# Text layers: scores in row groups of 64, gelu of two groups every second step, second norm one step later, variances on POOL

## The chip, the cores and the metric

The kernel runs on one core of a Trainium2 chip. The time is the device time of one execution in microseconds (us). A core has five engines that run side by side, each through its own list of instructions in order: PE (TensorE, matmuls; its weight loads are shown apart as PEld), DVE (VectorE), ACT (ScalarE), POOL (GpSimd) and SP (SyncE, here only transfers). They wait for each other by semaphores.

## What is computed

A block with four parts: an image branch (convolutions), a text branch of four transformer layers, then an attention over both and a layer of experts. The change touches only the text branch. Cut to that:

```python
L, H, D, F, V, S = (4, 8, 64, 256, 100, 512)
DH = D // H                       # 8
x = emb[tokens] + positional_encoding(Sq, D)[None]     # tokens (64, 77)
for i in range(L):
    q = (x @ Wq[i] + bq[i]).reshape(B, Sq, H, DH).transpose(0, 2, 1, 3)
    k = (x @ Wv[i] + bv[i]).reshape(B, Sq, H, DH).transpose(0, 2, 1, 3)
    v = (x @ Wv[i] + bv[i]).reshape(B, Sq, H, DH).transpose(0, 2, 1, 3)
    attn = jax.nn.softmax(jnp.einsum('bhqd,bhkd->bhqk', q, k) * scale, axis=-1)
    o = jnp.einsum('bhqk,bhkd->bhqd', attn, v).transpose(0, 2, 1, 3).reshape(B, Sq, D)
    x = x + layer_norm(o @ Wo[i] + bo[i], ln1_g[i], ln1_b[i])
    h = jax.nn.gelu(x @ W1[i] + b1[i], approximate=False)
    x = x + layer_norm(h @ W2[i] + b2[i], ln2_g[i], ln2_b[i])
return layer_norm(x, fin_g, fin_b)
```

## The kernel before

The function `text_branch` holds all of it. The 64 samples of 77 tokens are worked on in groups of four (`QUAD`), so 16 groups (`U`) and 4 layers make N = 64 pieces of work, numbered q. All of a group's activations stay in the core's memory.

**Heads.** The eight heads of 8 channels stand in two tensors (`t`), four heads in each; a head has 32 of the 128 rows (`GROUP` = 32, `HPT` = 4). In its 32 rows lie the channels in three parts (high and low parts of a split into two precisions) and a row for the maximum. To multiply one head alone with 128 rows, K is written four times by POOL (`split_k`, L1055) into `KB`, each copy with all rows but one head's set to zero (`head_rows` is the mask): 4 x 312 columns for each tensor.

**One sample's attention** is a chain over the engines: `score` (PE, L1318: two matmuls of 128 rows with 312 columns, four heads side by side) - `find_max` (DVE, L916, reads the scores from PSUM) - `turn_max` (PE, L1328, two transposes) - `join_max` (DVE, L926, puts the maximum into the rows of Q: `QP`) - `score_t` (PE, L1340: eight matmuls, one a head, 78 columns each) - `exp` (ACT, L1186) - `weigh` (PE, L1354: eight products with weights of 9 columns, placed in four column groups of the array; sixteen instructions in the profile) - `copy_outs` (ACT, L1192) - `turn_outs` (PE, L1362) - `normalise_o` (DVE, L936 and L938). `score` of the next sample waits for `find_max` of this one (one buffer), `weigh` of the next for `normalise_o` (one bank), `score_t` of the next for `exp`.

**Around it**, once a group: `hi_x`, `cut_x`, `turn_x` (L1261), `set_xT`, `project_k` (L1285), `project_q` (L1294), `project_v` (L1304), with `lo_k`, `lo_q` (ACT, L1170, L1177) and `cut_k`, `cut_q` (DVE, L886, L895) that split the results; `turn_o` (L1269), `project_o` (L1370, L1374), then the first norm: `square_a` (ACT), `var_a` (DVE: the sum L952 and the variance L956), `power_a` (POOL, L1079), `scale_a` (L947), `shift_a`, `sum_a` (L965). Then the feed-forward part: `hi_f`, `cut_f`, `turn_f` (PE, L1277), `set_fT`, `up` in two halves (PE, L1383), `gelu` in two halves (ACT, L1213), `down` (PE, L1393 and L1397), and the second norm in the same manner with `_y` (L980, L984, L1086, L975, L993).

**Order.** Each engine has a function `step(n)` in which the order is written out by hand; step n works on group n, n-1, ... n-5 at different points of the pipeline. There is no loop on the chip, all N + 5 steps are written out. ACT has to load a table before gelu and again before the next exp: two table loads in each step. PE's six projections share two PSUM banks:

```python
WORK = dict(x=1, k0=0, k1=1, q0=0, q1=1, v=1, o=0, a=0, f=1, up0=0, up1=1, y=0)
```

`take(use, read, q)` waits until the bank's last content was read: project_v and up of half 1 use bank 1, project_q of tensor 0 (read by `cut_q` on DVE) and up of half 0 use bank 0.

## Time and profile before

| | us |
|---|---|
| median of 3 runs | 2328.38 (2327.67 to 2330.51) |
| the profiled execution | 2329.04 |
| its span, first to last instruction | 2327.2 |

Busy over the whole span: PE 2091.1 (90%), DVE 1735.5 (75%), ACT 1419.1 (61%), POOL 1144.9 (49%). The text layers take the stretch from about 560 to 1445 us. "Idle before" in brackets is time in which the engine had nothing to run, and behind the arrow stands what ended it. Matmuls overlap, and their ends are modelled: the distance between the ends (start plus duration) of two neighbouring groups is the time that the later group takes up.

### The profile page before, as it was taken

The numbers are of one execution on the slowest core, as the hardware profiler recorded it, in microseconds if no ns is written. First come the engines' busy times: TensorE is split into PE (matmuls) and PEld (weight loads), VectorE is DVE, ScalarE is ACT, GpSimd is POOL, SyncE is SP. The second block draws the span as 40 slices with busy tenths as digits, with TensorE's granted clock in tenths as the row PEclk, the third lists the DMA queues.
The fourth block names the chain that finished last, engine by engine and source line by source line (L and its number), as shares of the span: only waits on it lengthen the run. The fifth ranks groups of instructions, "written<-read, shape, count | busy, mean of one in ns | idle before, by whom it ended". The sixth has DMA issues, their size and how long they took to land. (4 is left out here: it accounts for less than half of the span.)

```text
span 2327.2 us, 59267 instructions
## 1 busy us (share of the span) xinstructions
PE 2091.1 (90%) x20401; PEld 1720.2 (74%) x20401; DVE 1735.5 (75%) x5336; ACT 1419.1 (61%) x3034; POOL 1144.9 (49%) x1520
## 2 busy tenths in 40 slices
PE   5999999965999999999999997099999996999998
PEld 5999999954888888888888886066666664666665
DVE  4655555426788888888888885668888775888888
ACT  2222222211788888888888885466666665666663
POOL 4333333312577777777777774633333324343442
PEclk8999999975999999999999998589999996999999
DMA  2000003000000000000000000000000000000000
GB/s 91 16 15 14 14 14 81 13 1 0 2 3 2 3 2 3 2 3 2 3 2 3 2 3 1 0 1 2 2 2 2 2 1 3 10 9 9 9 9 11
DMA packets 38895, 21.14 MB, mean 9 GB/s; under 512 B 28696, under 2 KB 38040, under 8 KB 38554
## 3 DMA queue, kind: packets, MB, share of 16 engines
q1 hardware_dynamic: 38654, 17.97, 3.1%
q8 instruction: 146, 2.39, 0.4%
q14 instruction: 95, 0.78, 0.1%
HBM read 14.60 MB, written 3.36 MB: 8 GB/s over the span
## 5 line engine op out<-in xcount | busy, mean ns | idle before, releaser
L452 PE MATMUL im_c<-im_a_hi,im_w 128*128 128x256 f32 (+2 forms) x1920 | 427.0, 317 | 15.3 <-POOL im_a_lo L362 15.3
L452 PEld LDWEIGHTS im_c<-im_a_hi,im_w 128*128 128x128 f32 x1920 | 320.5, 190 | 32.4 <-POOL im_a_lo L362 15.5
L452 PE MATMUL im_c<-im_a_lo,im_w 128*128 128x256 f32 (+2 forms) x960 | 302.8, 315 | 0.0
L1055 POOL TENSOR_TENSOR tx_KB<-tx_KF,tx_head_rows 128x1248 fp32r<-128x1248 f32 x128 | 290.0, 2265 | 23.2 <-PE tx_scores_t L1340 15.2
L356 POOL TENSOR_TENSOR im_rstd<-im_var_eps,im_power 128x4 f32<-128x4 f32 x64 | 68.7, 1073 | 282.9 <-DVE im_var_eps L291 282.9
L916 DVE TENSOR_REDUCE tx_mpad<-tx_scores 77x8 fp32r<-77x616 f32 x256 | 202.1, 789 | 2.8 <-PE tx_maxT L1328 1.9
L285 DVE BATCH_NORM_STATS2 im_stats<-im_h 128x6 f32<-128x128 f32 (+1 forms) x192 | 47.6, 303 | 189.8 <-ACT im_h L397 110.7
L452 PEld LDWEIGHTS im_c<-im_a_lo,im_w 128*128 128x128 f32 x960 | 182.2, 190 | 8.3
L1186 ACT ACTIVATE tx_PT<-tx_scores_t 77x624 f32<-77x624 f32 x256 | 176.1, 688 | 16.8 <-PE tx_scores_t L1340 4.6
L1340 PE MATMUL tx_scores_t<-tx_QP,tx_KB 128*77 128x78 f32 x2048 | 183.9, 240 | 0.0
L1340 PEld LDWEIGHTS tx_scores_t<-tx_QP,tx_KB 128*77 128x77 f32 x2048 | 172.4, 150 | 9.1 <-issue 0.3
L2379 PE MATMUL ex_y<-ex_wd,ex_H_hi 128*128 128x512 f32 (+1 forms) x512 | 171.7, 416 | 0.0
L1768 DVE TENSOR_REDUCE at_mpad<-at_scores 128x4 fp32r<-128x820 f32 (+1 forms) x128 | 129.5, 1012 | 43.3 <-PE at_scores L1988 43.2
L1854 POOL TENSOR_TENSOR at_xs<-at_z,at_xs 128x128 fp32r<-128x128 f32 x64 | 29.4, 460 | 245.4 <-ACT at_xs L1871 245.4
L391 ACT ACTIVATE im_a_hi<-im_normed 128x192 fp32r<-128x192 f32 (+1 forms) x192 | 63.1, 349 | 139.3 <-DVE im_normed L309 137.0
L1047 POOL TENSOR_TENSOR tx_xs_f<-h,tx_xs_f 77x256 fp32r<-77x256 f32 x64 | 46.7, 730 | 199.9 <-ACT tx_xs_f L1136 199.9
L2268 DVE TENSOR_REDUCE ex_summed<-ex_weighted 128x64 f32<-128x512 f32 (+1 forms) x128 | 135.5, 1059 | 4.4
L1578 POOL TENSOR_TENSOR ex_rstd<-ex_var_eps,ex_power 128x2 f32<-128x2 f32 x64 | 44.6, 697 | 181.2 <-DVE ex_var_eps L1543 181.2
L1903 ACT ACTIVATE at_PT<-at_scores_t 128x824 f32<-128x824 f32 (+1 forms) x128 | 109.7, 857 | 30.7 <-PE at_scores_t L2011 26.9
L1318 PE MATMUL tx_scores<-tx_KB,tx_QF 128*77 128x312 f32 x512 | 126.0, 327 | 1.3 <-DVE tx_mpad L916 1.2
L1354 PE MATMUL tx_out_bank<-tx_PT,tx_V 128*9 128x78 f32 x4096 | 118.0, 233 | 9.2 <-DVE tx_o_rows L938 2.3
L362 POOL TENSOR_TENSOR im_a_lo<-im_normed,im_a_hi 128x192 fp32r<-128x192 f32 (+1 forms) x192 | 93.7, 518 | 52.4 <-ACT im_a_hi L391 52.4
(321 smaller groups left out, 6062.3 us busy)
## 6 DMA issues: line engine op xcount, KB each, us to landing
im_x<-x SPq DMA_DIRECT2D x16, 384.0 KB, 3.3
out<-h SPq DMA_DIRECT2D x32, 64.0 KB
tx_toks<-x_txt SPq DMA_DIRECT2D x1, 1925.0 KB
im_raw<-L_tok_conv_w SPq DMA_DIRECT2D x1, 1280.0 KB, 8.5
out<-h SPq DMA_DIRECT2D x32, 38.5 KB
im_raw<-L_tok_conv_w SPq DMA_DIRECT2D x1, 960.0 KB, 4.6
im_raw<-L_tok_conv_w SPq DMA_DIRECT2D x1, 640.0 KB, 5.8
tx_raw_W<-L_txt_W SPq DMA_DIRECT2D x2, 256.0 KB, 6.7
```

What stands on the lines that cost most here:

```text
L362: last = pool.tensor_tensor(a_lo[c][:, par, b, :, 2:2 + J], normed[:, b, 0:cols * J].rearrange("p (d j) -> p d j", d=cols), a_hi[c][:, par ...
L452: last = pe.matmul(acc[:, :, d0:d1], w[c][:, slot, part], img[:, b0_:b1_, d0 + shift:d1 + shift, kj:kj + J], start=opens, stop=closes)
L916: dve.tensor_reduce(mpad[0:R].rearrange("p t (j r) -> p t j r", r=GROUP)[:, :, :, 3 * DH], scores[0:R, :, 0:HPT * SP_TXT].rearrange("p t ( ...
L1055: pool.tensor_tensor(KB[:, q % 2, t], KF[:, t].bitcast(F32).unsqueeze(1).broadcast_to([P, HPT, QW]), head_rows[:].unsqueeze(2).broadcast_t ...
L1186: act.activation(PT[0:R, b % 2], scores_t[0:R, :, 0:HPT * SP_TXT], ACT.Exp, scale=SCALE)\
L1318: last = pe.matmul(scores[0:R, t, 0:HPT * SP_TXT], QF[:, q % 2, t, b, 0:R], k, start=True, stop=True)
L1340: last = pe.matmul(scores_t[0:R, t, j * SP_TXT:(j + 1) * SP_TXT], k, QP[:, b % 2, t], start=True, stop=True)
L1354: last = pe.matmul(outT[32 * j:32 * j + DH + 1, t], V[:, q % 2, b, t * HPT + j], PT[:, b % 2, t, j * SP_TXT:(j + 1) * SP_TXT], start=True, ...
L1768: dve.tensor_reduce(mpad[0:n, tile].rearrange("p t (j r) -> p j t r", r=A_GROUP)[:, :, :, 3 * A_DH], scores[0:n, :, 0:WIDE].rearrange("p j ...
L1903: act.activation(PT[0:n, tile], scores_t[0:n, :, 0:WIDE], ACT.Exp, scale=SCALE).then_inc(exped, 1)
L2268: dve.tensor_reduce(summed[0:n, tile], weighted[0:n, tile].rearrange("p e d -> p d e"), AX.X, ALU.add)\
L2379: last = pe.matmul(acc, h[:, slot, half, at:at + n], wd[:, part, half, 0:WIDE], start=False, stop=half == HALVES - 1 and h is H_lo)
```

## The change

1. `score` and `score_t` work with 64 of the 128 rows at a time (`ROWS` = 2 halves of `PAIR` = 2 heads). K is written twice instead of four times (`KB`, 2 x 312 columns). `score` is four matmuls of 64 rows with 156 columns, `score_t` eight of 64 rows with 78; halves `a` alternate and go to different banks. The layout of `scores`, `scores_t` and `PT` follows.
2. `up` and `gelu` are run for two groups (n-6 and n-5) in each even step and not at all in odd ones. `down` and the second norm move from n-5 to n-6; the pipeline has N + 6 steps.
3. The variances (`tensor_scalar` on 77x4) move from DVE to POOL (`var_eps_a`, `var_eps_y`), and two waits at the end of POOL's step go.

```diff
-        KB = sb("KB", [P, 2, TENSORS, HPT, QW], F32R)
-        PT = sb("PT", [P, 2, TENSORS, HPT * SP_TXT])
+        KB = sb("KB", [P, 2, TENSORS, PAIR, QW], F32R)
+        PT = sb("PT", [P, 2, ROWS, HPT * SP_TXT])
...
                         dve.wait_ge(a_squared, q + 1)
+                        if q >= 2:
+                            dve.wait_ge(a_var, q - 1)
                         dve.tensor_reduce(a_sums[:, q % 2], a_square[:, q % 2], AX.X, ALU.add).then_inc(a_summed, 1)
-                        dve.wait_ge(a_summed, q + 1)
-                        if q >= 2:
-                            dve.wait_ge(a_power, q - 1)
-                        dve.tensor_scalar(a_var_eps[:, q % 2], a_sums[:, q % 2], 1.0 / D, EPS, ALU.mult, ALU.add)\
-                            .then_inc(a_var, 1)
...
-                        pool.tensor_tensor(KB[:, q % 2, t], KF[:, t].bitcast(F32).unsqueeze(1).broadcast_to([P, HPT, QW]),
-                                           head_rows[:].unsqueeze(2).broadcast_to([P, HPT, QW]), ALU.mult)\
+                        pool.tensor_tensor(KB[:, q % 2, t], KF[:, t].bitcast(F32).unsqueeze(1).broadcast_to([P, PAIR, QW]),
+                                           head_rows[:].unsqueeze(2).broadcast_to([P, PAIR, QW]), ALU.mult)\
...
+                def var_eps_a(q):
+                    if live(q):
+                        pool.wait_ge(a_summed, q + 1)
+                        pool.tensor_scalar(a_var_eps[:, q % 2], a_sums[:, q % 2], 1.0 / D, EPS, ALU.mult, ALU.add)\
+                            .then_inc(a_var, 1)
...
-                    shift_y(n - 5)
+                    shift_y(n - 6)
                     cut_x(n)
                     split_k(n - 1, 0)
+                    var_eps_a(n - 4)
                     power_a(n - 4)
                     cut_o(n - 3)
-                    power_y(n - 5)
-                    let_sum_y(n - 5)
-                    let_sum_a(n - 4)
+                    var_eps_y(n - 6)
+                    power_y(n - 6)
...
                     lo_q(n - 1, 0)
-                    gelu(n - 5, 1)
-                    gelu(n - 5, 0)
+                    if n % 2 == 0:
+                        gelu(n - 6, 1)
+                        gelu(n - 6, 0)
+                        gelu(n - 5, 1)
+                        gelu(n - 5, 0)
...
                         for t in range(TENSORS):
-                            k = KB[:, q % 2, t].rearrange("p j (b s) -> p j b s", b=QUAD)[:, :, b]
-                            last = pe.matmul(scores[0:R, t, 0:HPT * SP_TXT], QF[:, q % 2, t, b, 0:R], k, start=True, stop=True)
+                            for a in range(ROWS):
+                                rows, wide = slice(a * P // ROWS, (a + 1) * P // ROWS), PAIR * SP_TXT
+                                k = KB[rows, q % 2, t].rearrange("p j (b s) -> p j b s", b=QUAD)[:, :, b]
+                                last = pe.matmul(scores[0:R, a, t * wide:(t + 1) * wide], QF[rows, q % 2, t, b, 0:R], k,
+                                                 start=True, stop=True)
...
                         for t in range(TENSORS):
-                            for j in range(HPT):
-                                k = KB[:, q % 2, t, j].rearrange("p (b s) -> p b s", b=QUAD)[:, b, 0:R]
-                                last = pe.matmul(scores_t[0:R, t, j * SP_TXT:(j + 1) * SP_TXT], k, QP[:, b % 2, t],
-                                                 start=True, stop=True)
+                            for j in range(PAIR):
+                                for a in range(ROWS):
+                                    rows, at = slice(a * P // ROWS, (a + 1) * P // ROWS), (t * PAIR + j) * SP_TXT
+                                    k = KB[rows, q % 2, t, j].rearrange("p (b s) -> p b s", b=QUAD)[:, b, 0:R]
+                                    last = pe.matmul(scores_t[0:R, a, at:at + SP_TXT], k, QP[rows, b % 2, t],
+                                                     start=True, stop=True)
```

PE's order, from project_q of tensor 0 (L1294, after the change L1296) to project_v (L1304, after it L1306). Before, in every step:

```order
L1294 MATMUL tx_work<-tx_xT,tx_w_all 128x312 x2
L1362 MATMUL tx_out_bank<-ident,tx_oU 77x128 x2
L1383 MATMUL tx_work<-tx_xTf,tx_w_all 128x312 x2
L1340 MATMUL tx_scores_t<-tx_QP,tx_KB 77x78 x8
L1318 MATMUL tx_scores<-tx_KB,tx_QF 77x312 x2
L1328 MATMUL tx_maxT<-ident,tx_mpad 128x77 x2
L1383 MATMUL tx_work<-tx_xTf,tx_w_all 128x312 x2
L1354 MATMUL tx_out_bank<-tx_PT,tx_V 9x78 x8
L1304 MATMUL tx_work<-tx_w_all,tx_xT 77x64 x8
```

PE's order in the same place after the change, in an even step (in an odd one the four rows of L1391, `up`, are not there):

```order
L1296 MATMUL tx_work<-tx_xT,tx_w_all 128x312 x2
L1370 MATMUL tx_out_bank<-ident,tx_oU 77x128 x2
L1391 MATMUL tx_work<-tx_xTf,tx_w_all 128x312 x2
L1347 MATMUL tx_scores_t<-tx_QP,tx_KB 77x78 x8
L1391 MATMUL tx_work<-tx_xTf,tx_w_all 128x312 x2
L1322 MATMUL tx_scores<-tx_KB,tx_QF 77x156 x4
L1333 MATMUL tx_maxT<-ident,tx_mpad 128x77 x2
L1391 MATMUL tx_work<-tx_xTf,tx_w_all 128x312 x2
L1362 MATMUL tx_out_bank<-tx_PT,tx_V 9x78 x8
L1391 MATMUL tx_work<-tx_xTf,tx_w_all 128x312 x2
L1306 MATMUL tx_work<-tx_w_all,tx_xT 77x64 x8
```

The second `up`, of half 0, has moved from behind `turn_max` to between `score_t` and `score`, and two more stand on either side of `weigh`.

POOL's order from the second `split_k` (L1055, after it L1052) to the end of the step, before (L1079 and L1086 are the powers, L1041 is `cut_o`):

```order
L1035 TENSOR_TENSOR tx_xs<-h,tx_xs 77x4x64
L1055 TENSOR_TENSOR tx_KB<-tx_KF,tx_head_rows 128x1248
L1079 TENSOR_TENSOR tx_a_rstd<-tx_a_var_eps,tx_power 77x4
L1041 TENSOR_TENSOR tx_os<-tx_o_rows,tx_os 77x4x64
L1086 TENSOR_TENSOR tx_y_rstd<-tx_y_var_eps,tx_power 77x4
```

After:

```order
L1032 TENSOR_TENSOR tx_xs<-h,tx_xs 77x4x64
L1052 TENSOR_TENSOR tx_KB<-tx_KF,tx_head_rows 128x624
L1074 TENSOR_SCALAR tx_a_var_eps<-tx_a_sums 77x4
L1082 TENSOR_TENSOR tx_a_rstd<-tx_a_var_eps,tx_power 77x4
L1038 TENSOR_TENSOR tx_os<-tx_o_rows,tx_os 77x4x64
L1087 TENSOR_SCALAR tx_y_var_eps<-tx_y_sums 77x4
L1095 TENSOR_TENSOR tx_y_rstd<-tx_y_var_eps,tx_power 77x4
```

Each power now has its variance right ahead of it on POOL, and the K product has half the columns.

## Rows read from the trace of the kernel before

**Rows 1.** Windows: from:to, length, busy PE PEld DVE ACT POOL, PEclk, DMA share, GB/s.
```profile
800.00:1000.00 200.00, 191.99 (x2670) 171.12 (x2670) 177.12 (x525) 177.56 (x361) 149.60 (x135) 1.00 0.01 2
...
800.94:814.28 13.34, 12.88 (x180) 11.48 (x178) 11.81 (x36) 11.85 (x25) 9.98 (x10) 1.00 0.01 4
```

**Rows 2.** Groups, 600 to 1380 us: count | busy us, mean ns | idle before.
```profile
L1055 POOL TENSOR_TENSOR tx_KB<-tx_KF,tx_head_rows 128x1248 fp32r<-128x1248 f32 x118 | 267.3, 2265 | 4.3 <-PE tx_scores_t L1340 4.3
...
L956 DVE TENSOR_SCALAR tx_a_var_eps<-tx_a_sums 77x4 f32<-77x4 f32 x58 | 54.7, 943 | 2.0
```

**Rows 3.** Time line of PE in one step (start us, duration us, group).
```profile
800.33 0.68 PE L1340 MATMUL tx_scores_t<-tx_QP,tx_KB 128*77 128x78 f32 x8
800.94 0.46 PE L1354 MATMUL tx_out_bank<-tx_PT,tx_V 128*9 128x78 f32 x16
801.33 0.49 PE L1277 MATMUL tx_work<-ident,tx_xs_f 77*128 77x77 f32 x4
801.62 0.50 PE L1318 MATMUL tx_scores<-tx_KB,tx_QF 128*77 128x312 f32 x2
801.95 0.30 PE L1328 MATMUL tx_maxT<-ident,tx_mpad 77*128 77x77 f32 x2
...
802.64 0.54 PE L1383 MATMUL tx_work<-tx_xTf,tx_w_all 128*128 128x312 f32 x2
803.01 0.68 PE L1340 MATMUL tx_scores_t<-tx_QP,tx_KB 128*77 128x78 f32 x8
803.57 0.52 PE L1318 MATMUL tx_scores<-tx_KB,tx_QF 128*77 128x312 f32 x2
803.93 0.30 PE L1328 MATMUL tx_maxT<-ident,tx_mpad 77*128 77x77 f32 x2
804.11 0.52 PE L1383 MATMUL tx_work<-tx_xTf,tx_w_all 128*128 128x312 f32 x2
...
805.29 0.71 PE L1304 MATMUL tx_work<-tx_w_all,tx_xT 128*77 128x64 f32 x8 [0.27 <-ACT tx_HT L1213]
...
806.64 1.26 PE L1397 MATMUL tx_work<-tx_w_all,tx_HT 128*77 128x64 f32 x16
807.74 0.44 PE L1261 MATMUL tx_work<-ident,tx_xs 77*128 77x77 f32 x4
808.28 0.46 PE L1354 MATMUL tx_out_bank<-tx_PT,tx_V 128*9 128x78 f32 x16
808.67 0.75 PE L1340 MATMUL tx_scores_t<-tx_QP,tx_KB 128*77 128x78 f32 x8
...
812.85 0.38 PE L1362 MATMUL tx_out_bank<-ident,tx_oU 128*77 128x128 f32 x2
813.31 0.53 PE L1285 MATMUL tx_work<-tx_xT,tx_w_all 128*128 128x312 f32 x2
```

**Rows 4.** Time line of DVE in the same step: join_max, find_max, cut_q.
```profile
802.29 0.32 DVE L926 TENSOR_TENSOR tx_QP<-tx_maxT,tx_QF 128x154 fp32r<-128x154 f32 x1 [0.30 <-PE tx_maxT L1328]
802.72 0.80 DVE L916 TENSOR_REDUCE tx_mpad<-tx_scores 77x8 fp32r<-77x616 f32 x1
803.44 0.53 DVE L895 SCALAR_TENSOR_TENSOR tx_QF<-tx_work,tx_cols_all,tx_qk_lo 128x312 fp32r<-128x312 f32 x1
```

**Rows 5.** Time line of ACT in the same step: table load and gelu.
```profile
803.33 1.28 ACT L1213 ACT_TABLE_LOAD   x1
804.63 0.93 ACT L1213 ACTIVATE tx_HT<-tx_work,tx_cols_all 128x312 f32<-128x312 f32 x2
```

**Rows 6.** Time line of PE in the attention stage: a 128-row group, then 64-row pairs.
```profile
1651.29 0.61 PE L72 MATMUL at_of_q<-warm_rows 128*128 128x512 bf16 x2
1651.83 0.42 PE L1988 MATMUL at_scores<-at_KF,at_QF 64*77 64x206 f32 x4
```

**Rows 7.** Groups of POOL: a variance of 128x2 elements in the attention stage.
```profile
L1837 POOL TENSOR_SCALAR at_var_eps<-at_mean_var 128x2 f32<-128x2 f32 x64 | 14.1, 220 | 5.0 <-DVE at_mean_var L1761 5.0
```

**Rows 8.** Time line of PE at the end of the text layers: the last down.
```profile
1439.54 2.26 PE L1397 MATMUL tx_work<-tx_w_all,tx_HT 128*77 128x64 f32 x16
```

60 lines of the change are left out of this document (33 added, 27 removed).

## The prediction

> **What bounds the kernel now.** I read the window table first. In the text layers, from about 600 to 1400 us, PE is busy for 96% of the time at a granted clock of 1.00, that is 2.4 GHz, and one step (one group of four samples in one layer) takes 13.34 us: PE 12.88, DVE 11.81, ACT 11.85, POOL 9.98 busy [rows 1]. There are 64 such steps. PE is the bound, but DVE and ACT have only some 1.5 us of air each, so PE's own time and its waits must both be followed. The change touches nothing outside this stage.
>
> Next, the time line of PE in one step [rows 3]. I take the distance between the ends of neighbouring groups (start plus duration). Call T0 the end of the last score_t of the step before, 801.01. Two things are to be seen. First, what the narrow matmuls of weigh (L1354, 128 x 9 weights, four side by side) cost when PE goes into and out of them. Four transposes after weigh end 0.42 after it (L1277), while four transposes after ordinary matmuls end 0.28 after them (L1261 after L1397): leaving the narrow form costs about 0.15 us. Second, few true waits: project_v (L1304) with 0.27 idle; weigh of sample 0 (L1354 at 808.28) ends 0.56 after the transposes, where 0.39 is normal, so 0.17 is a wait; project_k (L1285 at 813.31) ends 0.61 after its neighbour, where a pair of such matmuls behind transposes takes about 0.33 (0.30 to 0.40 for L1383), so 0.2 to 0.3 is a wait. With a tenth here and there I put PE's waits at 1.05 and its work at 12.29 us a step.
>
> **The change part by part: PE's work.** The form to be priced, two 64-row matmuls side by side, stands in the attention stage: after a 128-row group that ends at 1651.90, two pairs of 64 x 77 weights with 206 columns end at 1652.25, so 0.35 us including the way in [rows 6]. From it I work out, as estimates at 2.4 GHz: score (now two pairs of 156 columns instead of two matmuls of 312) 0.35 less twice 50 columns, 0.31, or 0.18 directly behind another 64-row group; score_t (now four pairs of 78 columns instead of eight matmuls) 0.35 plus two more weight loads of 0.07 (that is the spacing of the eight now: 0.51 for eight) less the shorter columns, 0.40. Today score_t ends 0.51 after an ordinary group and 0.68 after weigh (808.67), score 0.29 to 0.34 [rows 3]. So four score_t go from 2.24 to 1.62 (-0.62), and four score from 1.25 to 1.24, or 1.09 in a step where one follows score_t directly.
>
> Against that stand the ways out. Five groups in each step now follow a 64-row group and did not follow a change of form before (turn_max four times, turn_outs once); no row shows this way out, so I take the nearest, that out of weigh, 0.15; the one behind score_t saves 0.05 of it: +0.70. Its bounds are 0.08 and 0.2. Such a pair of prices (entry is in the 0.35 already) makes PE's work in an odd step 12.29 - 0.69 (no up) - 0.62 - 0.16 + 0.70, 11.52 us. In an even step there are four up instead of two: +0.76, of which 0.08 is because one stands between two 64-row groups; score and score_t -0.63; ways out +0.70; another 0.1 for the second group behind weigh: 13.22. The mean is 12.37, no less than the 12.29 of now. What the narrow rows save, the changes of form give back. The Trainium skill, page "TensorEngine Tiling (Array Packing)", section "Key Properties", says that a change of tiling mode (not just of tile) drains the TensorE; the trace agrees with the 0.15 us around weigh. The same page, section "Theoretical Speedup", has up to 2x for a contraction of 64 rows or less; taken alone it would take half of 3.49 us a step.
>
> **ACT, DVE, POOL.** The table loads (1.28 us each, two a step) are made every second step: ACT loses 1.28 us a step on average, but an even step has four gelu of 0.47 and both loads in one piece [rows 5]. POOL's KB product is half as long, 2.26 to about 1.2 us [rows 2], and that is worth nothing by itself: POOL is busy for only 9.98 of 13.34 us [rows 1]. The variance on DVE takes 0.94 us for 77x4 elements [rows 2], far over what such a thing needs, and it delays normalise_o and so weigh of sample 0: the 0.17 goes. On POOL it costs 0.22 [rows 7] twice; on y it stands ahead of power_y, for which sum_y waits: up to 0.2, in the even step.
>
> **The new waits, by a walk through a step.** In row order: turn_max of sample 0 ended at T0+1.24. After the change it ends at 1.45 (0.15 way out, 0.05 because DVE's find_max for sample 0 comes later: turn_outs before it ends 0.15 later and score_t 0.12 earlier). Then join_max starts 0.04 later, find_max of sample 1 starts 0.43 after that and takes 0.79, and PE may start score of sample 2 0.05 after its end [rows 4]: 1.49, 1.92, 2.71, 2.76. Today this is T0+2.56, exactly when PE starts it (803.57): there is no slack left on this chain now.
> In an odd step PE would be ready for score 2 at about 2.25, since there is no up and score_t is shorter. It waits 0.5. Behind find_max DVE has cut_q (0.45 to the next start) and normalise_o (0.44), so weigh of the last sample, which needs the output bank free, waits another 0.3. The wait at project_v goes, that at weigh 0 goes, that at project_k stays near 0.2. Waits 1.05, step 12.57.
> In an even step up of half 0 (bank 0, held until cut_q is done) stands ahead of score 2. cut_q ends at 2.64 + 0.53 = 3.17, up starts at 3.28, PE was ready at 2.75: 0.5 us. Then up of half 1 of the second group must wait for gelu of the first: lo_q, table load, gelu end at 4.35, up starts at 4.46, 0.2 late. weigh, up, project_v, down follow; exp of sample 0 comes behind four gelu, a copy and the second table load, at about 8.6, just when PE wants weigh 0 (8.66): nothing or 0.05. project_o 0.05, project_q 0.2 (sum_y behind power_y), project_k 0.2. Waits 1.29, step 14.51.
>
> **Sum.** Mean step (12.57 + 14.51) / 2 = 13.54 against 13.34: +0.20, times 64 is +13 us. The pipeline is one step longer: a further down at the low clock, 2.26 us [rows 8], and the variance on POOL, +2.5. Of the profiled execution (2329.04, span 2327.2) this makes 2344.5; against the median of 2328.38 it is **2344 us**, +0.7%. One wait misjudged by 0.15 us a step is 10 us, and the way out at 0.08 or 0.2 makes -22 or +16 us (5.5 of them a step), of which part goes into waits, since a later PE waits less: I halve it. Own range 2333 to 2363.
>
> **Rivals.**
> (1) Relief wins: faster, 0.27. In the walk the waits add up; if those behind the first one of a step lie under it (PE late at the first is no longer early at the next, since DVE and ACT have been given 1.1 and 1.28 us a step), then the even step keeps 0.5 us of waits and ends at 13.7, the odd one loses the wait at the last weigh and ends at 12.3: 13.0, -0.34 x 64 + 2.5, 2309. It decides once more than 0.24 us a step falls away of the 1.17 that I count. For it: the table loads and the 0.94 us variance are real, and ACT is 89% busy. Against: the chain turn_max, join_max, find_max has no slack now, and the change makes it longer.
> (2) They cancel: 13.30 a step, 2328, 0.13.
> (3) My forecast, slower by turning forms and the two new waits: 0.55.
> (4) The pairs don't run side by side in this stage, since score_t has weights of only 77 columns and 78 columns to move: score_t back at 0.51 plus the way in of 0.1, +0.8 a step, 2385: 0.04. Against it rows 6.
> (5) The matmuls of both kinds cost half and changes of form are hidden, as a mechanism of this kernel: 3.49 / 2 x 64, -112 us if nothing else waited, but the DVE chain would hold it: at best 12.3 a step (DVE 10.9 busy plus what it waits), 2265. 0.01. This is what the 2x of the Trainium skill, page "TensorEngine Tiling (Array Packing)", section "Theoretical Speedup", would make; no row of the trace shows it.
> A way out of the 64-row form of 0.05 us instead of 0.15 would bring the forecast down to no change.
>
> **Chances and range.** A measurement of this kernel tells about 0.2% (4.7 us) from no change. Slower 0.59 (3, 4), same 0.13, faster 0.28 (1, 5). The range, 2306 to 2368, takes in most of rival 1 and the bounds of the forecast.
>
> **What would show it.** PE's busy time near 96% with PE's groups turn_max behind score ending 0.28 to 0.30 after it instead of 0.13; score_t at 0.40 and four 64-row weight loads in pairs; odd and even steps of 12.6 and 14.5; idle time of PE ahead of score in odd steps put down to tx_mpad, and ahead of the first up of half 0 in even steps put down to tx_QF; no DVE variance, ACT busy near 80%. It is wrong if turn_max still ends 0.13 after score, or if the even step is under 13.8.

## The result, and the profile after

| | before | after |
|---|---|---|
| median, us | 2329.45 (2327.67 to 2333.0, 4 runs) | 2386.81 (2383.55 to 2391.64, 4 runs) |
| span of the profiled execution, us | 2327.2 | 2381.7 |

The ratio is 1.0246 (95% interval 1.0222 to 1.027): slower, by 57 us where the forecast had 16, and outside the range of 2306 to 2368. The ratios here and below compare fast runs with fast runs; one run of rows_pairs (2440.8 us) and one of rows_heat64_long (2365.8 us) were slow and are left out of theirs.

First the steady part: the window table of the changed kernel, with one odd and one even step on top, then three stretches that cover the start of the stage, then the first three steps one by one (columns as in [rows 1]):

```profile
831.11:843.74 12.63, 12.11 (x187) 9.71 (x183) 10.80 (x34) 8.44 (x21) 8.25 (x12) 1.00 0.01 2
843.74:858.45 14.71, 13.73 (x194) 10.87 (x190) 10.87 (x34) 12.56 (x27) 8.28 (x12) 1.00 0.01 2
...
561.00:591.00 30.00, 22.75 (x169) 17.05 (x169) 11.99 (x26) 12.41 (x24) 8.28 (x9) 0.50 0.00 1
591.00:620.00 29.00, 28.74 (x282) 23.28 (x281) 15.32 (x43) 13.27 (x28) 8.34 (x11) 0.50 0.00 1
620.00:673.00 53.00, 52.87 (x467) 42.81 (x467) 27.87 (x79) 28.23 (x57) 21.78 (x28) 0.50 0.01 2
...
624.00:641.61 17.61, 17.48 (x169) 13.95 (x165) 9.45 (x28) 8.81 (x20) 6.44 (x9) 0.50 0.01 3
641.61:664.00 22.39, 22.39 (x195) 18.33 (x191) 10.98 (x34) 13.95 (x27) 8.33 (x12) 0.50 0.01 1
664.00:679.60 15.60, 15.60 (x186) 12.89 (x182) 10.24 (x33) 8.27 (x21) 7.26 (x11) 0.70 0.01 2
```

An odd step takes 12.63 us and an even one 14.71 (14.72 in most), a mean of 13.675; the forecast had 12.57, 14.51 and 13.54. The two lower blocks are what the forecast did not speak of at all: TensorE's granted clock is 0.50 (1.2 GHz) from 561 to 673 us, while PE is busy for 28.74 of 29 and 52.87 of 53 us. The first two of these stretches in the kernel before:

```profile
561.00:591.00 30.00, 22.56 (x144) 19.24 (x148) 11.38 (x26) 11.53 (x23) 11.12 (x7) 0.50 0.00 1
591.00:620.00 29.00, 26.86 (x382) 23.55 (x375) 21.87 (x61) 20.32 (x44) 19.71 (x16) 1.00 0.01 2
```

There the clock goes to 1.00 (2.4 GHz) at 591.2, 82 us earlier. PE's time line at the end of this stage in the kernel before:

```profile
1447.03 0.77 PE L1277 MATMUL tx_work<-ident,tx_xs_f 77*128 77x77 f32 x4 [5.23 <-POOL tx_xs_f L1047]
...
1450.76 2.26 PE L1397 MATMUL tx_work<-tx_w_all,tx_HT 128*77 128x64 f32 x16
```

I mark a step by its first turn_f (four transposes of `tx_xs_f`); the first one of all starts at 614.7 before and at 624.0 after, and the last at 1447.03 and at 1496.31. The last sum_y (DVE adds the second norm of the last group) ends at 1456.1 and at 1510.9. So the 54.5 us between the two spans divide up like this:

| part of the text stage | us |
|---|---|
| up to the first turn_f, at half clock for longer | 9.3 |
| the first three steps, 17.61 + 22.39 + 15.60 against 3 x 13.33 | 15.6 |
| the other 60 steps: 56 at +0.34 (19), one of them with a short fall of the clock (1.6 more), and the last four, where the pipeline empties (4.1) | 24.4 |
| from the last turn_f to the last sum_y, 14.6 against 9.1 | 5.5 |
| the stages after | -0.3 |

The time line of PE in the changed kernel: pieces of the odd and of the even step, and the end of the stage (start, duration, group):

```profile
831.11 0.49 PE L1279 MATMUL tx_work<-ident,tx_xs_f 77*128 77x77 f32 x4
831.66 0.37 PE L1322 MATMUL tx_scores<-tx_KB,tx_QF 64*77 64x156 f32 x4
831.96 0.35 PE L1333 MATMUL tx_maxT<-ident,tx_mpad 77*128 77x77 f32 x2
832.20 0.52 PE L1296 MATMUL tx_work<-tx_xT,tx_w_all 128*128 128x312 f32 x2
832.56 0.38 PE L1370 MATMUL tx_out_bank<-ident,tx_oU 128*77 128x128 f32 x2
832.87 0.47 PE L1347 MATMUL tx_scores_t<-tx_QP,tx_KB 64*77 64x78 f32 x8
833.43 0.38 PE L1322 MATMUL tx_scores<-tx_KB,tx_QF 64*77 64x156 f32 x4
...
834.46 0.46 PE L1362 MATMUL tx_out_bank<-tx_PT,tx_V 128*9 128x78 f32 x16 [0.37 <-DVE tx_o_rows L941]
...
845.79 0.47 PE L1347 MATMUL tx_scores_t<-tx_QP,tx_KB 64*77 64x78 f32 x8
846.72 0.53 PE L1391 MATMUL tx_work<-tx_xTf,tx_w_all 128*128 128x312 f32 x2 [0.46 <-DVE tx_QF L897]
856.10 0.52 PE L1296 MATMUL tx_work<-tx_xT,tx_w_all 128*128 128x312 f32 x2 [0.31 <-DVE tx_KF L888]
...
1501.60 2.26 PE L1405 MATMUL tx_work<-tx_w_all,tx_HT 128*77 128x64 f32 x16
1505.20 0.47 PE L1401 MATMUL tx_work<-tx_w_all,tx_ones 128*77 128x256 f32 x1 [1.34 <-DVE tx_y_scaled L975]
1505.47 2.25 PE L1405 MATMUL tx_work<-tx_w_all,tx_HT 128*77 128x64 f32 x16
```

And DVE's find_max just ahead of the first of these scores:

```profile
830.82 0.79 DVE L918 TENSOR_REDUCE tx_mpad<-tx_scores 77x8 fp32r<-77x616 f32 x1
```

Read as ends of neighbouring groups: turn_max ends 0.28 behind score (832.03, 832.31), where it was 0.13 in [rows 3]; score_t ends 0.40 behind the transposes (832.94, 833.34). The score of sample 2 ends 0.47 behind score_t, where the prediction's estimate is 0.18 without a wait. So it waits 0.29, and the forecast had 0.5. Another 0.13 stands one score earlier: that of sample 1 ends 0.43 behind turn_f (831.60, 832.03) instead of 0.30, and starts 0.05 behind the end of find_max (831.61). weigh of the last sample (834.46) waits 0.37 for normalise_o, where the forecast had 0.3. In the even step the first up of half 0 (846.72) waits 0.46 for cut_q (forecast 0.5), and project_q (856.10) waits 0.31 for cut_k (forecast 0.2). ACT is busy for 21.0 of the 27.34 us of the two steps, 77%; the forecast had near 80.

### The profile page after: what moved, and what is told of

It reads as the page before. It is cut to its first block and busy times, and to the rows that moved or that the text cites. A ratio compares the mean times of both kernels' runs of the same rounds, so it can differ in the third digit from the quotient of the medians.

```text
span 2381.7 us, 60100 instructions
## 1 busy us (share of the span) xinstructions
PE 2130.4 (89%) x20849; PEld 1680.4 (71%) x20913; DVE 1676.5 (70%) x5208; ACT 1338.8 (56%) x2972; POOL 1034.6 (43%) x1648
## 5 line engine op out<-in xcount | busy, mean ns | idle before, releaser
L1052 POOL TENSOR_TENSOR tx_KB<-tx_KF,tx_head_rows 128x624 fp32r<-128x624 f32 x128 | 156.8, 1225 | 27.7 <-PE tx_scores_t L1347 17.9
L1362 PE MATMUL tx_out_bank<-tx_PT,tx_V 128*9 128x78 f32 x4096 | 123.0, 240 | 12.2 <-DVE tx_o_rows L941 10.9
L1347 PE MATMUL tx_scores_t<-tx_QP,tx_KB 64*77 64x78 f32 x2048 | 125.8, 250 | 0.3 <-DVE tx_QP L929 0.2
L1347 PEld LDWEIGHTS tx_scores_t<-tx_QP,tx_KB 64*77 64x77 f32 x2048 | 95.0, 151 | 40.0 <-issue 22.2
L1176 ACT ACTIVATE tx_qk_lo<-tx_work,tx_cols_all,tx_lo_rows 128x312 fp32r<-128x312 f32 x128 | 78.2, 611 | 67.9 <-PE tx_work L1296 64.0
```

Source lines behind the costliest of these rows:

```text
L1052: pool.tensor_tensor(KB[:, q % 2, t], KF[:, t].bitcast(F32).unsqueeze(1).broadcast_to([P, PAIR, QW]), head_rows[:].unsqueeze(2).broadcast_ ...
L1176: act.activation(qk_lo[:, t], bank(f"q{t}")[:, 0:QW], ACT.Identity, bias=col(q, 2 + t), scale=lo_rows[:, 0:1]).then_inc(q_lo_[t], 1)
L1347: last = pe.matmul(scores_t[0:R, a, at:at + SP_TXT], k, QP[rows, b % 2, t], start=True, stop=True)
L1362: last = pe.matmul(outT[32 * j:32 * j + DH + 1, t], V[:, q % 2, b, t * HPT + j], PT[:, b % 2, j // PAIR, at:at + SP_TXT], start=True, stop ...
```

## The experiments

The steady step, in us, is the distance between turn_f in the trace of each kernel; times are medians of all runs of a kernel. R is part 1 of the change (row groups of 64), P part 2 (two groups every second step, second norm six steps behind), V part 3 (variances on POOL). Ratios are to the kernel before, run beside each; its own median moved between the sets of runs, from 2328.7 to 2333.4 us, so compare ratios and not times.

| kernel | step odd / even | mean | time, us | ratio, 95% interval |
|---|---|---|---|---|
| before | 13.33 | 13.33 | 2329.45 | 1 |
| rows_only (R) | 13.10 | 13.10 | 2334.6 | 1.0012 (1.0 to 1.0024) |
| var_only (V) | 13.74 | 13.74 | 2352.48 | 1.0089 (1.007 to 1.0109) |
| pairs_only (P) | 13.27 / 14.43 | 13.85 | 2367.2 | 1.0146 (1.0127 to 1.0166) |
| rows_var (R, V) | 13.10 | 13.10 | 2328.54 | 1.0004 (0.9981 to 1.0027) |
| rows_pairs (R, P) | 12.63 / 14.56 | 13.60 | 2414.15 | 1.035 (1.0278 to 1.0422) |
| pairs_var (P, V) | 13.75 / 14.56 | 14.15 | 2391.85 | 1.0252 (1.0231 to 1.0272) |
| after (all) | 12.63 / 14.72 | 13.68 | 2386.81 | 1.0246 (1.0222 to 1.027) |
| rows_heat | 13.10 | 13.10 | 2330.04 | 1.0004 (0.9994 to 1.0014) |
| before_heat | 13.33 | 13.33 | 2326.16 | 0.9983 (0.9974 to 0.9993) |
| after_heat | 12.63 / 14.72 | 13.68 | 2403.18 | 1.0327 (1.0298 to 1.0355) |
| rows_heat64 | 13.10 | 13.10 | 2332.65 | 1.0015 (1.0006 to 1.0025) |
| rows_heat_long | 13.10 | 13.10 | 2329.18 | 0.9976 (0.995 to 1.0002) |
| after_up0 | 12.63 / 14.72 | 13.68 | 2386.22 | 1.0239 (1.0194 to 1.0283) |
| rows_heat_both | 13.10 | 13.10 | 2329.01 | 0.9981 (0.997 to 0.9993) |
| before_heat_both | 13.33 | 13.33 | 2348.61 | 1.0024 (0.9991 to 1.0056) |
| after_heat_long | 12.63 / 14.72 | 13.68 | 2376.77 | 1.0209 (1.0141 to 1.0277) |
| rows_heat64_long | 13.10 | 13.10 | 2318.21 | 0.9937 (0.9915 to 0.9959) |
| rows_heat64_long again | 13.10 | 13.10 | 2322.52 | 0.9938 (0.9915 to 0.9962) |
| after_short_gelu | 12.63 / 14.34 | 13.49 | 2391.75 | 1.024 (1.0206 to 1.0274) |

### The parts one by one

Part 1 alone. The edit is every line of the change on `KB`, `head_rows`, `PT`, score, score_t and find_max; the order of work is that of before.

```diff
-        KB = sb("KB", [P, 2, TENSORS, HPT, QW], F32R)
+        KB = sb("KB", [P, 2, TENSORS, PAIR, QW], F32R)
...
+                            for a in range(ROWS):
+                                rows, wide = slice(a * P // ROWS, (a + 1) * P // ROWS), PAIR * SP_TXT
```

> The kernel before with the first part of the change alone: 64-row groups in score and score_t, half the K product; orders, gelu and variances as before. Theory A: it is the 64-row matmuls that keep TensorE at its 1.2 GHz level longer at the start of the text layers (after the change it rose at 673 us, before at 591). Then the clock rises late here too, between 650 and 690 us, which costs 20 to 30 us, and the steady step is 13.3 to 13.6 us: 2350 to 2375 us. Theory B: the late clock comes from the uneven steps (up and gelu every second step). Then it rises near 591 us here and the time is 2328 to 2345.

Windows of this kernel, one steady step, then the start of the stage:

```profile
810.57:823.66 13.09, 12.83 (x187) 10.25 (x187) 11.11 (x36) 11.86 (x25) 7.91 (x10) 1.00 0.02 4
...
591.00:620.00 29.00, 28.75 (x283) 23.21 (x282) 14.83 (x44) 13.41 (x29) 7.06 (x8) 0.50 0.00 1
620.00:673.00 53.00, 51.96 (x669) 41.73 (x669) 39.86 (x124) 44.13 (x86) 29.47 (x34) 0.86 0.01 2
```

Two of its groups from 640 to 1380 us (count | busy us, mean ns | idle before):

```profile
L1058 POOL TENSOR_TENSOR tx_KB<-tx_KF,tx_head_rows 128x624 fp32r<-128x624 f32 x114 | 139.6, 1224 | 0.0
...
L959 DVE TENSOR_SCALAR tx_a_var_eps<-tx_a_sums 77x4 f32<-77x4 f32 x56 | 9.3, 166 | 1.9
```

The step is 0.23 us shorter: PE is busy for 12.83 us, nearly what it was (12.88, [rows 1]), and what went are its waits. The variance on DVE, 943 ns in [rows 2], takes 166 ns here although its line is untouched. What changed is what runs beside it. In the kernel before, DVE's variance of the first norm starts while POOL's KB product is running, and ends just behind it (807.77 against 807.75):

```profile
805.49 2.26 POOL L1055 TENSOR_TENSOR tx_KB<-tx_KF,tx_head_rows 128x1248 fp32r<-128x1248 f32 x1
...
806.82 0.95 DVE L956 TENSOR_SCALAR tx_a_var_eps<-tx_a_sums 77x4 f32<-77x4 f32 x1
```

From 600 to 1380 us all 58 of these variances meet the product and end 22 to 103 ns after it (median 24), while the 57 of the second norm, which meet none, take 172 ns. In rows_only, with a product of 1224 ns, none of the 58 meets it. (In pairs_only, shown below, 29 of 56 do and take 1339 ns, and the other 27 take 166.) So the variance does not take long: it is held until POOL's product is over. How much of the 0.23 us this alone is worth no run separates, since part 1 also changes PE's matmuls and POOL's load.

Neither theory had this kernel. The step is below A's 13.3 to 13.6, but the clock rises at 634.5, between B's 591 and A's 650 to 690; the first turn_f comes at 622.9 and the first step takes 17.36: the seventh turn_f is 11.2 us late (705.8 against 694.6), and 60 shorter steps just pay that back.

Part 3 alone: `tensor_scalar` on 77x4 moves to POOL, the two waits at the end of POOL's step go, nothing else.

```diff
-                        dve.tensor_scalar(a_var_eps[:, q % 2], a_sums[:, q % 2], 1.0 / D, EPS, ALU.mult, ALU.add)\
-                            .then_inc(a_var, 1)
...
+                    var_eps_y(n - 5)
```

> The kernel before with the third part alone: both variances on POOL. Both theories: clock rises near 591 us. DVE loses 0.94 and 0.17 us a step and the 0.17 us that PE waits ahead of weigh of sample 0 go: step 13.1 to 13.3 us, 2315 to 2329 us. If POOL's power_y, which comes 0.2 us later, is what DVE then waits for, the step stays 13.3.

The waits of this kernel from 700 to 1380 us (engine, line, releaser: us in total, times, longest):

```profile
DVE h L987 <- POOL tx_y_rstd L1092: 33.0, 50, 0.7
...
PE tx_work L1290 <- DVE tx_KF L886: 29.2, 49, 0.6
```

POOL's time line at the end of one of its steps:

```profile
837.21 2.26 POOL L1049 TENSOR_TENSOR tx_KB<-tx_KF,tx_head_rows 128x1248 fp32r<-128x1248 f32 x1
839.55 0.19 POOL L1071 TENSOR_SCALAR tx_a_var_eps<-tx_a_sums 77x4 f32<-77x4 f32 x1
839.83 1.01 POOL L1079 TENSOR_TENSOR tx_a_rstd<-tx_a_var_eps,tx_power 77x4 f32<-77x4 f32 x1
```

With the long products still on POOL, its queue sets the end: sum_y on DVE waits 0.66 us a step for `y_rstd`, cut_k stands behind sum_y, and PE's project_q waits 0.6 for cut_k. The step is 0.40 longer, though DVE has less to do; the expectation was 13.1 to 13.3, and it missed.

Part 2 alone: `up` and `gelu` of two groups in even steps, `down` and the second norm at n-6, variances on DVE.

```diff
-                    up(n - 5, 0)
+                    if n % 2 == 0:
+                        up(n - 5, 1)
```

> The kernel before with the second part alone: up and gelu for two groups every second step, second norm six steps behind; matmuls of 128 rows as before. Theory A: clock rises near 591 us, odd steps about 12.7 and even ones about 14.1 us, mean 13.4 and one more step at the end: 2330 to 2342 us. Theory B: the clock rises late (650 us or more), 2350 to 2370 us.

This is where the steady loss is: 0.52 us a step, where theory A had 0.1. The clock rises at 592.7, as theory A had it; the time is in theory B's range all the same, because of the step. The longest of PE's own waits from 700 to 1380 us is that for normalise_o:

```profile
PE tx_out_bank L1357 <- DVE tx_o_rows L938: 22.3, 50, 0.6
```

Part 2 was not taken apart further here: it pairs the activations, moves one `up` and delays the second norm, all at once.

Parts 2 and 3 together, then 1 and 3, then 1 and 2 (each edit is the sum of the pieces above):

> The changed kernel without its first part: second and third part on the kernel before, matmuls of 128 rows. Theory A: clock near 591 us, mean step 13.2 to 13.4 us, 2322 to 2337 us, so nearly all of the loss of 57 us is in the first part. Theory B: the clock rises late and the time is 2345 us or more.

> Parts 1 and 3 of the change without part 2: scores in row groups of 64 and the second norm six steps behind with its variances on POOL; each step activates its own group. Theory A (the pairing of the activations is the steady loss, the variances on POOL cost nothing once POOL's row groups have shortened its row products): the steady step is 13.0 to 13.2 us, as with the row groups alone (13.10), the clock rises late as there, and the time is 2328 to 2338 us. Rival B (POOL's chain binds as it did with the variances alone, where DVE's sum_y waited 0.66 us for tx_y_rstd in a step): the step is 13.4 to 13.6 us and the time 2350 to 2362 us.

> Parts 1 and 2 of the change without part 3: scores in row groups of 64 and the activations of two groups in every second step; the variances stay on DVE. Theory A (the pairing costs what it cost alone, 0.52 us a step, on top of the 0.235 that the row groups give, and part 3 adds nothing): the mean of an odd and an even step is 13.5 to 13.7 us, the clock rises late, and the time is 2375 to 2390 us, that of the whole change. Rival B (the whole change loses by its part 3 too, since POOL carries the variances): the mean step is 13.3 to 13.4 us and the time 2355 to 2368 us.

With these all combinations of the three parts are there. pairs_var was expected at 2322 to 2337 us by theory A, and took 2392 with the clock up at 592.4: the loss is not in part 1 alone. Beside part 1, part 3 is worth nothing either way (13.10 with and without). That fits with the variance on DVE being short already, and with POOL having room once the products are short. Part 2 costs 0.50 to 0.58 us a step in three of its four pairings (13.85 - 13.33, 13.60 - 13.10, 13.68 - 13.10) and 0.41 beside part 3 alone. Part 3 on top of parts 1 and 2 adds 0.08. Yet rows_pairs takes longer than the whole change with a shorter step: three of its runs took 2403 to 2424 us, and the one in the trace has a span of 2403.0 against 2381.7. Its windows tell why:

```profile
1110.70:1138.00 27.30, 27.30 (x238) 22.80 (x231) 14.23 (x44) 15.24 (x29) 10.60 (x12) 0.50 0.01 2
1421.30:1448.60 27.30, 27.30 (x238) 22.79 (x231) 14.24 (x44) 15.23 (x29) 10.58 (x12) 0.50 0.01 1
```

The clock falls to 1.2 GHz twice in mid-stage for 27.3 us, with PE busy all the time, and an odd and an even step take 18.79 and 18.38 us instead of 27.19 together: +10 each time. The shorter falls in this trace (6.8 us at 752.3, 3.4 us at 1083.4 and 1394.0) add some 6 more; less the shorter steps, that makes the 21 us.

### The clock at the start

"heat" puts two more bf16 matmuls of 128x512, whose results nobody reads, ahead of each turn_x, project_k, project_q, project_v and score of the first two steps, and twelve ahead of the stage.

```diff
+                def heat(n, times=2):
+                    if n < 2:
+                        for _ in range(times):
+                            pe.matmul(scores_t[:, 0], warm.rows[:, 0:P], warm.rows[:], start=True, stop=True)
...
+                heat(0, 12)
```

> Row groups alone (rows_only) plus 52 matmuls of 128 rows with 512 bf16 columns that compute nothing used, 12 ahead of the text layers' first step and two ahead of the larger groups of the first two steps, mostly where PE waited. Theory C: the steady step is a gain (13.10 against 13.33) and only the clock at the start takes it back; dense 128-row work raises the clock by 575 us and 64-row groups then keep it up. Then the clock rises at 565 to 580 us and the time is 2303 to 2315 us. Theory D: with 64-row groups the clock falls back once the extra matmuls are over; the time stays above 2328.

> The kernel before plus the same 52 matmuls. Clock rises at 565 to 580 us instead of 591; 2 or 3 steps at the high level instead of the low one, less what the extra matmuls delay: 2315 to 2325 us, steady step unchanged at 13.33. So if rows_heat is well below this, the row groups are a gain by themselves.

> The changed kernel plus the same 52 matmuls. If the late clock (673 us) is worth what the trace says, about 4 steps of 20 instead of 13.7 us, the time falls by 20 to 30 us, to 2355 to 2368, and the rest, 27 to 40 us over the kernel before, is the steady step of 13.67 us and the longer end. If it falls by under 10 us, the clock is not what costs.

The same extra work lifts the clock at 559.5 to 561.6 us in all three. In before_heat it stays up (seventh turn_f at 692.1 against 694.6, 0.17% gained in all). With the row groups it falls back at 580, 3.3 us after the last of the extra matmuls (576.6), and rises where it rose without them, 634.5. In after_heat it comes back only at 696 and falls once more, at 1389 for 27.3 us, which is why that kernel is slower than the changed one. By its own measure this test went against the clock as the cause (the time was to fall by 20 to 30 us and rose by 16); the trace shows that it didn't bring about what it was to test. So a start alone is not enough: with the row groups, the stream of the first steps doesn't hold the clock that the extra work won.

Is it that 64-row matmuls don't count? The same with each extra matmul replaced by two of 64 rows side by side:

```diff
+                            for a in range(2):
+                                half = slice(a * 64, (a + 1) * 64)
+                                pe.matmul(scores_t[:, a], warm.rows[half, 0:P], warm.rows[half], start=True, stop=True)
```

> As rows_heat, but each extra matmul is a pair of 64-row matmuls side by side (same 512 columns, same time). Theory E: what holds the clock down is the 64-row form itself, also in a dense stream. Then the clock rises later than with 128 rows, at 600 us or after, and the time is 2318 to 2335. Theory F: it is the holes in PE's stream around each change of form, or LDWEIGHTS share, not the rows. Then the extra pairs raise the clock as early as rows_heat does, and the two times agree within 4 us.

They raise the clock at 561.4, as the tall ones do, and it falls and rises again at 581.9 and 636.5, against 579.9 and 634.5. In work as dense as this (512 columns each) the 64-row form doesn't keep the clock from rising. Next, the extra work kept up for longer: three more matmuls in each score_t of the first two groups (q below 2), up to about 602 us, on rows_heat, on after_heat, and in the 64-row form on rows_heat64.

```diff
+                        if q < 2:
+                            for _ in range(3):
+                                pe.matmul(scores_t[:, 0], warm.rows[:, 0:P], warm.rows[:], start=True, stop=True)
```

> The row groups alone with the extra matmuls ahead of the stage, and three more matmuls of 128x512 in each score_t of the first two query tiles, whose results nobody reads. Theory A (the clock stays at 1.2 GHz because TensorE's stream in the first steps is not dense enough, and stays up once the stream is kept dense for that long): full clock from about 560 us on without a fall, the first turn_f below 614 us, steps of 13.1 us from the end of the extra work on, and 2315 to 2324 us. Rival B (the clock falls back when the extra matmuls are over, whenever that is): a second stretch of 1.2 GHz after them, up to about 634 us, and 2328 to 2336 us.

> The changed kernel with the extra matmuls ahead of the text stage and three more in each score_t of the first two query tiles. Theory A (about 25 us of the loss come from the clock that rises 82 us later at the start, 9 of them ahead of the first turn_f and 15 in three long steps): full clock from about 560 us on, first turn_f at 613 to 616 us, no long step, and 2355 to 2366 us, with the steady steps of 12.63 and 14.72 as they were. Rival B (the clock falls again as with the short extra work, which made the changed kernel slower): over 2380 us.

after_heat_long is the test of the 25 us. Its windows:

```profile
561.00:591.00 30.00, 26.11 (x229) 15.03 (x229) 13.34 (x29) 12.84 (x25) 9.53 (x11) 1.00 0.00 1
591.00:620.00 29.00, 26.86 (x409) 19.98 (x407) 21.30 (x60) 17.31 (x41) 12.90 (x16) 1.00 0.01 2
...
700.00:1327.00 627.00, 592.09 (x8524) 471.75 (x8522) 497.13 (x1515) 482.47 (x1056) 379.34 (x506) 1.00 0.01 2
1327.20:1354.50 27.30, 27.30 (x238) 22.80 (x230) 13.69 (x41) 15.22 (x29) 11.08 (x15) 0.50 0.01 2
```

The clock is up from 559.2, the first turn_f starts at 613.5 and the seventh at 694.7, where the changed kernel has 721.7 and the kernel before 694.6. These 27 us, all that was lost up to there, came back, and the steady steps are as they were. The span is 2363.2, with one fall of the clock at 1327 in it that costs 9.8. Of its four runs two took 2365 us, as theory A had it, and two 2388 and 2397. The mean granted clock of a whole run is 0.944 in the first two and 0.932 and 0.928 in the others, so those had more of the low clock; where, no trace shows.

rows_heat_long holds the clock from 561.5 on, has steps of 13.1 from the first, and ends the text stage at 1445.4, 10.7 us ahead of the kernel before (1456.1). But its ten runs fall into two heaps, three at 2314 and seven at 2329 to 2331. In the trace, which is one of the latter, the clock rises in the attention stage at 1544.6 and not at 1529.9 as before: what was won is given back there. So I put 24 more matmuls into the set-up of that stage, where PE stood idle:

```diff
                     last.then_inc(turned, 1)
+                    warm.run(pe, scores_t[:, 0], 24)
```

> The row groups alone with the long extra work at the start of the text stage, and 24 more matmuls of 128x512 in the set-up of the attention stage, where TensorE stood idle for 11.4 us, whose results nobody reads. Theory A (the 10.7 us that the row groups won by the end of the text stage were given back because the clock rose at 1544.6 instead of 1530 in the attention stage): full clock from about 1500 us on, and 2298 to 2313 us in all runs. Rival B (the clock falls back once the extra matmuls are over, as it did with the short extra work): a second stretch of 1.2 GHz to about 1545, and 2325 to 2332 us.

> The kernel before with the extra matmuls ahead of the text stage and the same 24 in the set-up of the attention stage: the part of the time of the other kernel that has nothing to do with the row groups. Theory A (the row groups are worth 0.23 us a step once the clock is the same in both): 12 to 15 us longer than the row groups with both heatings, 2310 to 2325 us. Rival B (the row groups are worth nothing): the two within 4 us.

PE's time line of rows_heat_both at that place:

```profile
1488.65 7.50 PE L72 MATMUL at_scores_t<-warm_rows 128*128 128x512 bf16 x24
1500.16 0.60 PE L1974 MATMUL at_x_and_k<-ident,at_xs 128*128 128x128 f32 x2 [4.01 <-POOL at_xs L1883]
```

Its windows there:

```profile
1490.00:1500.00 10.00, 6.15 (x22) 2.29 (x20) 7.59 (x43) 0.31 (x1) 4.64 (x13) 0.84 0.00 0
1500.00:1510.00 10.00, 7.68 (x30) 5.12 (x31) 2.88 (x8) 3.40 (x8) 3.90 (x10) 0.50 0.00 0
1510.00:1530.00 20.00, 20.00 (x112) 12.47 (x112) 10.16 (x24) 9.62 (x17) 4.31 (x10) 0.50 0.00 1
```

The clock does rise at 1493.0, and falls at 1499.9 while PE waits 4 us for POOL; then it stays at 0.50 with PE busy for 20.00 of 20 us, up to 1544.2. Theory A falls: the extra work that ended before this gap bought no time. before_heat_both is worse still, its clock rises at 1574.6 in the trace, and its runs lie at 2324, 2329 to 2330 and 2348 to 2351. The medians differ by 20 us, but since the cause is this rise and not the step, the pair doesn't price the row groups; the steps of 13.10 and 13.33 do.

> As the row groups with the long extra work, with each extra matmul of 128 rows replaced by two of 64 rows side by side, the form that the row groups brought. Theory A (what keeps the clock up is that TensorE has no gaps in the first steps, whatever the height of its matmuls): full clock from about 561 us on without a fall, and the time of the kernel with the 128-row extra work, 2314 to 2331 us. Rival B (64-row matmuls do not hold the clock in this stream): a second stretch of 1.2 GHz up to about 635 us, and 2330 to 2340 us.

> The kernel with the row groups and the long extra work of 64-row matmuls once more, for a trace of a run like those that took 2316 to 2318 us. Theory A (in those the clock stays up through the start of the text stage): full clock from about 560 us on, steps of 13.1 us after the extra work, and a median of 2315 to 2322 us. Rival B (the clock falls at about 607 us in these runs too, and they win in the attention stage): a stretch of 1.2 GHz after the extra work, with a first turn_f at 617 us or later.

These two are one kernel. The trace of the first was of an execution unlike its other six (2365.8 us against 2316 to 2324), so I read that of the second. In the odd one the clock was at 0.50 from 606.9 to 705.9. The second is of a run of 2323.1; its seven runs are again in two heaps, three at 2315 and four at 2323, and no trace shows the faster one:

```profile
561.30:609.10 47.80, 43.05 (x515) 27.01 (x512) 24.65 (x61) 21.46 (x45) 15.37 (x17) 1.00 0.01 1
609.10:629.60 20.50, 20.50 (x185) 17.01 (x186) 10.39 (x30) 12.94 (x25) 8.19 (x10) 0.50 0.01 2
...
629.60:1428.30 798.70, 772.12 (x11288) 615.55 (x11287) 666.42 (x2128) 717.37 (x1451) 477.17 (x543) 1.00 0.01 2
1428.30:1523.90 95.60, 25.81 (x127) 18.98 (x132) 48.99 (x265) 36.97 (x93) 49.09 (x89) 0.50 0.00 0
```

The clock falls at 609.1 after all, as rival B had it, but for 20.5 us only; the text stage ends at 1450.4, 5.7 us ahead of before, and the clock is back at 1523.9 in the attention stage, 6 us earlier than before, so nothing is given back (span 2321.3 against 2327.2). The ratio is 0.994 both times, the lowest of the study. Part of it is the kernel before, whose medians beside these two were 2333.4 and 2332.8 us and not the 2328.7 to 2329.7 of the other sets: against its lowest runs there (2327.6 and 2327.5) the two medians are 0.996 and 0.998. before_heat and rows_heat_both are ahead by 0.2%, also clear of 1.

And the height of the extra matmuls does show here. After the long extra work of 64 rows the clock fell at 606.9 and 609.1 in both traces, for 99 us and for 20.5; after the same work of 128 rows (rows_heat_long, rows_heat_both, after_heat_long) it did not fall there in any of three. Five traces are few, but the height is not ruled out.

### The even step

One entry moved: the first half of the older group's `up` stands behind the scores again.

```diff
-                    if n % 2 == 0:
-                        up(n - 6, 0)
                     score(n - 2, 2)
                     turn_max(n - 2, 1)
+                    if n % 2 == 0:
+                        up(n - 6, 0)
```

> The changed kernel with one entry moved: the first half of the up projection of the older group stands behind the scores again and not ahead of them, where TensorE waited for DVE's copy of the queries. Theory A (the scores queued behind that wait are what the even step loses): the even step falls from 14.72 to 14.2 to 14.4 us and the time by 10 to 16 us, to 2370 to 2377 us. Rival B (ACT's and DVE's work for two groups bounds the even step, wherever the half stands): 14.6 to 14.8 us and 2383 to 2392 us.

Rival B, with 14.72, to the hundredth what it was. The wait for cut_q is gone from ahead of `up`, and another has come ahead of an `up`, for gelu. From its waits between 800 and 1300 us:

```profile
PE tx_work L1391 <- ACT tx_HT L1212: 13.2, 18, 0.7
```

The clock rose at 654.5 here and not at 673.3, which made the start some 7 us shorter (seventh turn_f at 714.8 against 721.7). A late fall of 20.5 us, where the changed kernel has one of 3.4, took most of that back. Then each gelu cut from 312 columns to 78, which leaves three quarters of the gelus out of the computation:

```diff
-                        act.activation(HT[:, q % 2, half], bank(f"up{half}")[:, 0:QW], ACT.Gelu, bias=col(q, 8 + half))\
+                        wide = QW if q < 2 else QW // QUAD
+                        act.activation(HT[:, q % 2, half, 0:wide], bank(f"up{half}")[:, 0:wide], ACT.Gelu, bias=col(q, 8 + half))\
```

> The changed kernel with each activation of the feed-forward cut to the first 78 of its 312 columns from the third query group on (the other columns keep older values, so that part of the computation is left out): four activations of 0.52 us in each even step become about 0.3 us. Theory A (the even step waits on ScalarE's queue, in which four activations and a table load now stand in one run ahead of the copies and exponentials that TensorE waits for): the even step falls from 14.72 us to 13.8 to 14.2 us, the odd one stays at 12.63, and the time falls by 15 to 30 us. Rival B (TensorE's own work and DVE's copies make the even step): 14.5 to 14.75 us and 2380 to 2390 us.

A gelu takes 0.33 us and not 0.52, so ACT's even step is 0.78 lighter, and the step falls by 0.38, to 14.34. That is between the two theories: half of what ACT is given comes through, so the work on ACT is part of what makes the even step, and not all of it. And the kernel took no less time (2391.75): the clock rises at 695.7, and falls for 3.4 us in the trace again and again, each time with an odd step of 14.2 instead of 12.63.

## Why the prediction was wrong, point by point

- **The direction was right, and neither sign of being wrong came** (turn_max still 0.13 behind score, or an even step under 13.8). The size was wrong, and not by a price of the steady step.
- **The sizes of PE's pieces held.** turn_max 0.28 behind score (0.28 to 0.30 forecast), score_t 0.40, score 0.29 to 0.31 where it doesn't wait, 0.46 ahead of `up` half 0 (0.5 forecast). The Trainium skill's rule that was cited there, page "TensorEngine Tiling (Array Packing)", section "Key Properties", agrees: a way out of the 64-row form costs 0.15 us here behind score and 0.10 behind score_t. Its 2x (section "Theoretical Speedup") is in no run: four score_t went from 2.2 to 1.60 us, 1.4 times, before the ways out are counted.
- **The walk held too**: 12.57 and 14.51 forecast, 12.63 and 14.72 measured. The 0.135 in the mean are 8 us over the stage. Part 3 is not where it missed: it adds 0.16 to the even step (14.56 in rows_pairs, 14.72 with it), and the forecast had up to 0.2. It fits a little better than it should: the waits listed in it add up to 1.0 and 1.2 us, where the sum uses 1.05 and 1.29. From the list the mean would be 13.47 and the time some 4 us less. The wait ahead of score 2 was 0.29 and not 0.5, with 0.13 more ahead of score 1. Also, "5.5 of them a step" doesn't go with the -22 and +16 us, which are those of five.
- **What a part gives was right only for the sum.** I counted the row groups as no gain (12.37 of work against 12.29). Alone they take 0.23 off a step. With them DVE and POOL have less to do, and the variance on DVE takes 0.17 instead of 0.94 us, because it no longer stands behind POOL's long product. I gave part 3 that gain; it comes with part 1 already, and alone part 3 loses 0.40 through POOL's queue. My statement that the shorter KB product "is worth nothing by itself" had a reason that failed: POOL is busy for only 10 of 13.3 us, but its long product holds up DVE's variance, and what stands at the end of its queue is waited for.
- **The step of the forecast that failed is the sum**, "+0.20, times 64". It takes every step at the steady rate and puts the time that TensorE's clock needs to rise at the start of the stage at nothing, without a reason. The first three steps took 15.6 us more and the way to the first turn_f 9.3, 25 us together, at a granted clock of 0.50 that lasts 82 us longer. The row groups alone bring 43 of these 82 us (591.2 to 634.5); no part without them moves the rise by more than 1.5 us (590.0 to 592.7 in var_only, pairs_only and pairs_var). With the clock held up in after_heat_long, the seventh turn_f is back where the kernel before has it.
- **The end was undersized**: +5.5 behind the last turn_f for the +2.5 of the sum, and 4.1 in the last four steps, where +0.20 each makes 0.8. The last two groups of `up`, gelu and `down` now run one behind the other at 1.2 GHz with nothing beside them, and between the two downs PE waits 1.34 us for the scaling of the first: one more down was priced, its chain wasn't.
- **Rival 1** (relief wins) falls: the waits did not melt into each other. Rival 4 gave 2385, near the time, by a mechanism that isn't there: the pairs do run side by side. Its nearness is luck.

Not settled: what in the stream decides when the clock rises. PE's busy share does not tell: in the last 12.2 us ahead of the rise in the kernel before PE was busy all the time, and so it was after the change for 28.74 of 29 and 52.87 of 53 us without a rise. The height of the matmuls is open too: short and dense, the 64-row ones raise the clock as the others do, but after the long extra work it fell only with them. Kernels with part 2 have falls of the clock in mid-stage, seven of 3.4 us in the trace of pairs_var, but pairs_only has none; why, and why the long ones of 27.3 us come in some traces and not in others, is open as well.

## What to carry to other kernels

Sum a change over the stage as it runs, start and end included: a change of form that costs nothing in the steady step can move the moment at which the clock rises, and here that cost more (25 us) than the steady steps did (19 us). Bundling work of two iterations into one can lengthen that iteration by more than it shortens the other, where engines wait for each other in a ring: here 1.28 us of table loads a step were saved and 0.5 us a step lost. And try the parts of a change apart: one of the three was a gain of 0.23 us a step, one became harmless only beside the first, and one was the loss.

## What the runs showed of the hardware

- The granted clock stayed at 1.2 GHz (0.50) with PE busy for 81.6 of 82 us (591 to 673 us after the change). In rows_heat it rose at the same instant as in rows_only, 634.5, though extra work had lifted it in between; in after_heat it rose later than after the change (696.1 against 673.3).
- In mid-stage it fell from 2.4 GHz with PE busy 92 to 96% of the time (592.09 of 627 us in after_heat_long, 154.05 of 167.30 in pairs_var): for 27.3 us in rows_pairs (twice), after_heat and after_heat_long, at a cost of 10 us each, and for 3.4 us in others, at 1.6 us each in the changed kernel.
- A DVE operation on 77x4 elements took 943 ns in the kernel before, where all 58 of them ran into POOL's 2265 ns product and ended right behind it (median 24 ns), and 166 ns in rows_only, where none met it. On POOL itself it took 189 ns (L1074 of the changed kernel).
